# Three small moves in a four-stage transformer kernel: a side product over all 128 rows, the second norm's statistics later, the last outputs ahead of the last values

## The reference

```
x = x + tanh(g_xattn[0]) * autocorrelation(layernorm(x), ctx, ctx)
x = x + tanh(g_ffn[0])   * routed_lora_linear(layernorm(x), W, b, A, B, gate_w, gate_b)
x = x + tanh(g_xattn[1]) * grouped_query_attention(layernorm(x), ctx, ctx, mask, wq, wk, wv, wo)
x = x + tanh(g_ffn[1])   * (layernorm(x) @ W_base.T + b_base + 0.5 * update)
```

## Time and profile before

| | us |
|---|---|
| median of 3 runs (lowest, highest) | 3059.48 (3057.39, 3059.80) |
| the profiled execution | 3057.99 |
| its span | 3056.2 |
| TensorE busy in it | 2994.0 |
| VectorE busy in it | 1979.1 |
| ScalarE, GpSimd busy in it | 1252.7, 1271.8 |
| mean granted clock of TensorE | 0.993 of 2.4 GHz |

### The profile page before, as it was taken

The page is one execution under the profiler, slowest core; times in us unless marked ns, Lnnn a source line. Parts: engine busy times, 40 slices in busy tenths (PEclk is TensorE's granted clock), DMA queues, the critical chain, the costliest instruction groups (busy, mean ns, idle before and its releaser), DMA issues.

```text
span 3056.2 us, 40952 instructions
## 1 busy us (share of the span) xinstructions
PE 2994.0 (98%) x14752; PEld 2504.6 (82%) x14752; DVE 1979.1 (65%) x4642; ACT 1252.7 (41%) x2626; POOL 1271.8 (42%) x1028
## 2 busy tenths in 40 slices
PE   9999999999999999999999899999999999999999
PEld 7888778887777878878888788888888888888787
DVE  4432478887665686678667867666766676666432
ACT  4111466675333322242224455644544544544210
POOL 2422388886322577778775333311111111111231
PEclk9999999999999999999999999999999999999999
DMA  7332421113555654455444766765566556575321
GB/s 246 127 124 97 167 57 63 69 56 116 171 192 190 197 158 111 110 153 157 110 111 142 222 228 223 245 209 176 184 202 201 181 166 226 182 274 171 116 93 56
DMA packets 317461, 479.91 MB, mean 157 GB/s; under 512 B 26108, under 2 KB 155516, under 8 KB 315468
## 3 DMA queue, kind: packets, MB, share of 16 engines
q1 hardware_dynamic: 316540, 475.84, 48.8%
q10 hardware_dynamic: 720, 1.44, 0.1%
HBM read 319.92 MB, written 157.29 MB: 156 GB/s over the span
## 4 chain that ended last, share of the span: by engine, by line
PE 58%; DVE 5%; ACT 1%; DMA 1%; issue 0%; POOL 0%; SPq 0%; ACTq 0%; DVEq 0%
PE PB L150 18%; PE PB L151 18%; PE PB L152 18%; PE PB L2380 3%; DMA at_wol<-wod 1%; DVE qp_r L2178 1%; PE PB L2679 0%; DVE qp_b L2141 0%; DVE at_ptl L2519 0%; ACT at_ss L2427 0%; DVE PB L2181 0%; DVE at_ss L2499 0%; DVE qp_r L2186 0%; DVE qp_c L2183 0%; DVE qp_r L2179 0%
## 5 line engine op out<-in xcount | busy, mean ns | idle before, releaser
L2542 POOL TENSOR_TENSOR at_ql<-at_qf,at_qh 128x512 fp32r<-128x512 f32 x128 | 166.2, 1299 | 915.5 <-ACT at_qh L2420 915.5
L2427 ACT ACTIVATE at_ss<-at_ss,at_sm,at_bs 128x256 f32<-128x256 f32 x512 | 301.9, 591 | 336.5 <-DVE at_sm L2503 336.5
L150 PE MATMUL PB<-at_woh,at_ah 128*128 128x512 f32 x1024 | 402.2, 393 | 5.1 <-POOL at_wol L2549 3.4
L151 PE MATMUL PB<-at_wol,at_ah 128*128 128x512 f32 x1024 | 401.1, 392 | 0.0
L152 PE MATMUL PB<-at_woh,at_al 128*128 128x512 f32 x1024 | 400.3, 391 | 0.0
L2533 DVE SCALAR_TENSOR_TENSOR at_xt<-PB,gt,at_xt 128x512 f32<-128x512 f32 x256 | 192.1, 750 | 260.6 <-PE PB L152 260.6
L150 PE MATMUL PB<-qp_b,qp_a 128*128 128x512 f32 x896 | 350.8, 392 | 7.2 <-DVE qp_r L2184 3.7
L151 PE MATMUL PB<-qp_b,qp_a 128*128 128x512 f32 x896 | 350.1, 391 | 0.0
L152 PE MATMUL PB<-qp_b,qp_a 128*128 128x512 f32 x896 | 350.1, 391 | 0.0
L2208 POOL TENSOR_TENSOR qp_a<-qp_raw,qp_a 128x512 fp32r<-128x512 f32 x192 | 259.7, 1364 | 102.2 <-ACT qp_a L2103 99.6
L2439 ACT ACTIVATE at_pth<-PB 128x512 fp32r<-128x512 f32 x256 | 139.2, 596 | 242.4 <-PE PB L2380 242.4
(11 more groups left out here) (290 smaller groups left out, 7459.5 us busy)
## 6 DMA issues: line engine op xcount, KB each, us to landing
at_woh<-wod SPq DMA_DIRECT2D x48, 1024.0 KB, 6.4
at_wol<-wod SPq DMA_DIRECT2D x48, 1024.0 KB, 9.0
qp_raw<-in_wq SPq DMA_DIRECT2D x32, 1024.0 KB, 5.3
qd<-qp_r SPq DMA_DIRECT2D x256, 128.0 KB, 2.5
at_qf<-qd SPq DMA_DIRECT2D x128, 256.0 KB, 3.5
at_rawo<-in_wo SPq DMA_DIRECT2D x32, 512.0 KB, 5.3
wod<-at_woh SPq DMA_DIRECT2D x16, 1024.0 KB, 5.5
wod<-at_wol SPq DMA_DIRECT2D x16, 1024.0 KB, 6.3
```

What stands on the lines that cost most here:

```text
L150: pe.matmul(o, ah, bh, start=start, stop=False)
L151: pe.matmul(o, ah, bl, start=False, stop=False)
L2427: m = act.activation(at_ss[s][:, c, :], at_ss[s][:, c, :], ACT.Exp, bias=z[:, 4 + c:5 + c], scale=at_bs[:, qn % 2, 8 + 2 * b + c % 2:9 + 2 ...
L2542: self.pool.tensor_tensor(at_ql[n % 3][:, :], at_qf[n % 2][:, :], asf(at_qh[n % 3][:, :]), ALU.subtract).then_inc(*inc("at_pool", ("q", n)))
```

## The change

Three edits. A: the second matmul of each side piece takes all 128 rows of both operands, so that it also adds the encoders' low part times the spectrum's low part. B: on VectorE `stats2` of the odd tiles 3 to 13 moves from the end of its pair's steps to `begin` of the next pair, behind the low part of `flip(t+2)` and ahead of `stats(t+4)`; tile 15 keeps its place. C: in step u = 129 of attention `output(31, 1)` goes ahead of `values(127)`, on all engines (it has work on TensorE and VectorE).

```diff
@@ f0_tensor, piece
                         pe.matmul(BK[4 + hf], f0_er[:, cs], f0_uth[:, halves(hf)], start=True, stop=False)
-                        m = pe.matmul(BK[4 + hf], f0_er[0:64, cs], f0_utr[0:64, halves(hf)], start=False, stop=True)
+                        m = pe.matmul(BK[4 + hf], f0_er[:, cs], f0_utr[:, halves(hf)], start=False, stop=True)
@@ f0_vector, begin
                 lora_flip(t)
                 if t + 2 < NT:
                     flip(t + 2)
-                    if t + 4 < NT:
-                        stats(t + 4)
+                if t > 2:
+                    stats2(t - 1)
+                if t + 4 < NT:
+                    stats(t + 4)
                 piece(2 * t)
@@ f0_vector, end
                 piece(2 * t + 3)
                 leave(t + 1)
-                stats2(t + 1)
+                if t + 2 == NT:
+                    stats2(t + 1)
@@ at_schedule
                 if 1 <= u < NU + 1:
                     do.weigh(u - 1)
+                if u == NU + 1:
+                    do.output(m, 2 * k + 1)
                 if 2 <= u < NU + 2:
                     do.values(u - 2)
-                if u > 4:
+                if u > 4 and u != NU + 1:
                     do.output(m, 2 * k + 1)
```

## The result

| | before | after |
|---|---|---|
| median of 8 runs each, us | 3057.98 | 3068.18 |
| lowest to highest, us | 3052.61 to 3061.23 | 3064.81 to 3073.71 |
| the profiled execution, its span, us | 3057.99, 3056.2 | 3071.86, 3070.1 |

The ratio is 1.0036, with a 95% interval of 1.0025 to 1.0048: the change costs 11 us (8 to 15). 3073 had been forecast, with a range of 3062 to 3080. The profiled execution of after is a long one of its kind: its span grew by 13.9 us, where the sum said 13.8.

A forecast was written before the change was run, and what follows sets the result against it. TensorE, busy 98% of the span, was taken to bound the kernel. Terms: 12.4 (B's waits) + 8.0 (clock) - 3.1 (A) - 3.5 (C) = +13.8 us on 3057.99, so 3071.8; forecast 3073 for the runs, range 3062 to 3080.

The forecast's parts named there:

- A, the size of a piece: Side product: 128 rows save 0.78 us a piece; four of eight pieces only lengthen waits, so 3.1 us gained.
- B, no gain: VectorE, flip's low part: comes no earlier, since the statistics ran in time free while waiting for ScalarE.
- B, the waits: First feed-forward, t = 4 to 14: TensorE waits for the chain or queue behind the moved statistics, 12.4 us lost.
- The clock: Behind five new TensorE waits over 2.33 us the granted clock falls, 1.6 us each: 8.0 us lost.
- What GpSimd does at t = 14: First feed-forward, GpSimd: add_bias and the qp preparation move by no more than TensorE does.
- C: Attention's hand-over to the last stage: the 3.96 us wait is filled, about 1.1 us for bank 5 appears; 3.5 us gained.
- the clock that holds throughout: First feed-forward and `lora_in` waits: new waits cost their own length only; 3065 us, chance 0.13.
- the hidden statistics: turn(t-1) in mid(t): moved statistics stay hidden, only A and C count; 3052 or 3049 us, chance 0.06.
- the side product without a saving: Side product: the long pitch is the side operands' own, so nothing is saved; 3076 us, chance 0.05.
- the hand-over without a gain: Attention's hand-over: the bank wait and a fallen clock eat the filled wait; 3076 us, chance 0.08.
- rival 5: Behind the moved statistics more is late: ScalarE's qp expansions at t = 14, or t = 6's clock; 3078 to 3083, chance 0.08.
- Rival 3: Side product saves nothing, 3076 us, chance 0.05; against it: only what follows the first 64-row matmul is late.

The follow-up runs named there:

- edit A alone: Kernel before with only the second side matmul over all 128 rows: ratio 0.9995 (0.9986 to 1.0004), median 3055.84 against 3056.83 us.
- B alone: Kernel before with only the odd tiles' second-norm statistics moved: ratio 1.0059 (1.0046 to 1.0072), median 3074.70 us.
- B in two pairs: Kernel before with the odd tiles' statistics moved for t = 10 and t = 12 only: ratio 1.0032 (1.0020 to 1.0044).
- the filled waits: Changed kernel plus matmuls nobody reads ahead of turn(9), turn(11) (12 each) and turn(13) (10): ratio to before 1.0028 (1.0018 to 1.0038).
- A and C: Kernel before with the 128-row side matmul and output(31, 1) ahead of values(127), statistics not moved: ratio 0.9982 (0.9974 to 0.9991), median 3051.89 us.
- 64 rows: Kernel before with both side matmuls over rows 0 to 63 only: ratio 1.0004 (0.9995 to 1.0013).
- even tiles: Edits A and C without B, stats2(t) of even tiles moved from mid(t) to odd(t), behind flip(t+3)'s low part: ratio to before 0.9971, median 3048.06 us.
- C alone: Kernel before with only output(31, 1) put ahead of values(127): ratio 0.9988 (0.9979 to 0.9997), 3.7 us less (1 to 6).

## Why the prediction was right, point by point

- **A, the size of a piece**: 0.78 us forecast, 0.78 in the profile. That only four pieces count is shown by edit A alone: the f0 distance is 1.3 us less and not 6.2, and the two waits grew by 1.6 us each.
- **B, no gain**: shown by the 0.22 us that the low part still waits, and by the free time ahead of it that grew.
- **B, the waits**: 3.0 us forecast at turn(9) and turn(11), 2.84 and 2.85 measured; 2.4 and 2.33 at turn(13); 0.9 and 0.74 at turn(3); 3.2 and 2.98 at the two `lora_in`. Those at the turns come from a chain of 4.2 us that measured 4.17, those at the `lora_in` from VectorE's queue, as reckoned. B alone and B in two pairs show that the statistics' place does it.
- **The clock**: the mechanism is right, as the filled waits show. The term, 5 x 1.6 = 8.0 us, fits the profiled execution in sum only, and by luck. Behind four of the waits its price can be read against an execution in which the clock held at the same place. It was 2.7 us behind `lora_in(8)` (11.63 us to turn(6), against 8.89 with edit A alone), 1.5 behind `lora_in(10)` (10.43 to turn(8), against 8.92 with A and C), 1.6 behind turn(9) and 1.3 behind turn(11). The fifth fall cost the stage nothing. Together that is 7.1 us.
- **What GpSimd does at t = 14**: the prediction let its preparation of the queries move by no more than TensorE does. It moved by 3.2 us more, and 1.3 us of the loss between turn(13) and turn(15) are its doing and not the clock's. The forecast had 1.6 us of clock there, so the sum came out.
- **How often the clock falls**: the prediction had it fall each time. At these places there are 20 waits of 2.2 to 3.4 us in seven profiles (the change 5, A 2, B 5, A and C 2, two pairs 2, the `lora_in` of the filled kernel 2, 64 rows 2), and it fell behind 15; behind those of 1.8 to 2.0 us at the two `lora_in` (before, C, two pairs, even tiles) it fell once in 8. At three in four the term is, as an estimate, 5 x 0.75 x 1.6 = 6.0, and the whole 11.8, beside the 11 of the ratio. But its interval, 8 to 15, holds 13.8 as well, so the times don't decide between the two; only the profiles show that the clock does not always fall.
- **C**: 3.5 us forecast, 3.8 in the profile and 3.7 by the runs of C alone. Both remaining waits (1.2 and 1.1 forecast, 1.24 and 1.07 measured) stand where they were put, and the clock stayed up.
- **The rivals**: the clock that holds throughout, the hidden statistics, the side product without a saving and the hand-over without a gain each fall by a row above. Of more being late behind the statistics (rival 5), turn(5) and turn(7) waited 1.58 us, but that was swallowed by the next wait, and turn(14) became late by 1.3 us, on GpSimd. Rival 3's reading that only what follows the first 64-row matmul is late is not quite what the rows say: that matmul is late itself, by 0.32 us in place of 0.23.

## What to carry to other kernels

Before an instruction is moved behind another, ask of both who waits for them and how long they had been ready: here the one that was let ahead never waited for the engine, and the one that was moved had 0.8 us of slack for 3.8 us of delay. The same move paid where the waits and the slack lay the other way round. A saving ahead of a wait on another engine's chain only lengthens the wait, and can lose the clock besides.

## What the runs showed that I had not expected

The clock behind equal waits differs: 1.00 and 0.57 behind 3.39 and 3.40 us in one execution, 0.63 and 1.00 behind two of 2.85 us in another. Nor is it a matter of the place: behind `lora_in(8)` it stayed up with edit A alone and fell (0.61) with A and C, after waits of 3.39 and 3.38 us. Nor is there a length that is safe among those seen: it fell once behind 1.81 us. And a fall is not of one size: the granted clock was 0.50 for 6 us behind `lora_in(8)` in the changed kernel, and low for some 3 us behind the others. What decides it was not tried. It may be part of why executions of one kernel spread over 9 us here, which is argued and not shown.
